# The gate product of the first attention moved ahead of the last convolution tap of q

## The reference, cut to what matters

```
q = _silu(x @ Wq); k = _silu(x @ Wk); v = _silu(x @ Wv); z = x @ Wz
q = _causal_dwconv(q, conv_q_w)          # 4 taps; k and v likewise
q = q * cos + rot_half(q) * sin          # k likewise
q = q / max(norm(q), 1e-12)              # k likewise
for s in range(4):                       # k, v and a, lagged by s tokens
    attn = sum_d(q * k_s) / sqrt(D)
    out = out + (attn * sigmoid(a_s * b))[..., None] * v_s
out = out * rsqrt(mean(out * out) + eps) * norm_w * _silu(z)
return out @ Wout
```

## Time and profile before

| | |
|---|---|
| median of 3 runs | 1179.99 us |
| profiled execution | 1189.32 us |
| its span | 1187.5 us |
| mean granted TensorE clock | 0.924 |
| TensorE matmuls busy | 1043.6 us, 88% of the span |
| VectorE busy | 750.1 us, 63% |
| ScalarE busy | 552.7 us, 47% |
| the product L1333 | 16 times, 112.2 to 436.6 us |

### The profile page before, as it was taken

The page is one execution under the profiler, slowest core; times in us unless marked ns, Lnnn a source line. Parts: engine busy times, 40 slices in busy tenths (PEclk is TensorE's granted clock), DMA queues, the critical chain, the costliest instruction groups (busy, mean ns, idle before and its releaser), DMA issues.

```text
span 1187.5 us, 16824 instructions
## 1 busy us (share of the span) xinstructions
PE 1043.6 (88%) x5771; PEld 819.4 (69%) x5771; DVE 750.1 (63%) x1275; ACT 552.7 (47%) x1081; POOL 285.7 (24%) x243
## 2 busy tenths in 40 slices
PE   6788999999999959847976999999997997669986
PEld 4567888888888844323434988998897454458775
DVE  1378998998989819953125787778776134523344
ACT  1056777777778648910113555555554021122220
POOL 0004234243243310022002112211210005336560
PEclk8589999999999969968997999999998998689997
DMA  7037778777677760060001111111100102168744
GB/s 259 1 86 155 165 157 167 156 158 173 153 152 168 186 139 10 1 186 9 0 0 46 36 54 53 45 34 53 53 0 0 67 1 75 52 204 257 248 154 183
DMA packets 77373, 121.59 MB, mean 102 GB/s; under 512 B 25027, under 2 KB 54414, under 8 KB 76560
## 3 DMA queue, kind: packets, MB, share of 16 engines
q1 hardware_dynamic: 65296, 86.91, 24.1%
q0 software_dynamic: 12032, 34.11, 15.0%
HBM read 70.31 MB, written 38.08 MB: 91 GB/s over the span
## 4 chain that ended last, share of the span: by engine, by line
PE 65%; DVE 19%; issue 6%; ACT 5%; DMA 3%; POOL 1%; DVEq 1%; another core or an unknown queue 0%; POOLq 0%; ACTq 0%; SPq 0%
PE psum L604 7%; PE psum L606 7%; PE psum L605 7%; PE psum L838 5%; PE psum L964 5%; DVE arena L1313 4%; PE psum L924 4%; PE psum L627 4%; PE psum L811 3%; PE psum L704 3%; PE psum L656 2%; DVE arena L1408 2%; PE psum L974 2%; PE psum L757 2%; PE psum L589 2%
## 5 line engine op out<-in xcount | busy, mean ns | idle before, releaser
L1313 DVE SCALAR_TENSOR_TENSOR arena<-arena,par_in 128x1024 f32<-128x1024 f32 x144 | 184.6, 1284 | 40.4 <-ACT arena L1041 28.2
L604 PE MATMUL psum<-lut_w_r,arena_r 128*128 128x512 f32 x320 | 132.0, 413 | 17.0 <-POOL arena_r L1739 10.1
L605 PE MATMUL psum<-lut_w_r,arena_r 128*128 128x512 f32 x320 | 127.7, 399 | 0.0
L606 PE MATMUL psum<-lut_w_r,arena_r 128*128 128x512 f32 x320 | 127.6, 399 | 0.0
L1723 POOL DMA_DIRECT2D arena<-arena x64 | 53.8, 983 | 216.5 <-DVE arena L1325 216.4
L1142 ACT ACTIVATE arena<-psum,small 128x256 f32<-128x256 f32 x128 | 59.4, 473 | 85.8 <-DVE small L1450 85.8
L1031 ACT ACTIVATE arena<-psum 128x1024 f32<-128x1024 f32 x48 | 49.3, 1027 | 73.9 <-PE psum L606 73.4
L604 PEld LDWEIGHTS psum<-lut_w_r,arena_r 128*128 128x128 f32 x320 | 61.3, 192 | 30.2 <-issue 10.1
L604 PE MATMUL psum<-arena_r 128*128 128x256 f32 x256 | 77.7, 304 | 1.5 <-DVE arena_r L1475 1.5
L1770 POOL DMA_INDIRECT out_rows<-arena x64 | 62.8, 981 | 51.6 <-issue 20.8
L1739 POOL TENSOR_TENSOR arena_r<-arena,arena_r 128x512 fp32r<-128x512 f32 x16 | 21.2, 1325 | 216.9 <-ACT arena_r L1153 216.9
(11 more groups left out here) (228 smaller groups left out, 2404.0 us busy)
## 6 DMA issues: line engine op xcount, KB each, us to landing
arena<-arena POOLq DMA_DIRECT2D x64, 256.0 KB, 5.6
arena<-in_w_moe SPq DMA_DIRECT2D x33, 384.0 KB, 7.2
slot_rows<-nowhere SPq DMA_DIRECT2D x16, 576.0 KB, 4.3
arena<-slot_rows SPq DMA_DIRECT2D x32, 288.0 KB
arena<-bands SPq DMA_DIRECT2D x16, 528.0 KB, 4.4
sq_rows<-arena POOLq DMA_DIRECT2D x16, 512.0 KB, 7.3
arena<-in_w_qkvz SPq DMA_DIRECT2D x16, 384.0 KB, 3.3
arena<-in_qkv_codes SPq DMA_DIRECT2D x16, 384.0 KB, 3.2
```

What stands on the lines that cost most here:

```text
L604: nc.tensor.matmul(dst, w_l, x_h, start=start, stop=False, skip_group_check=True)
L605: nc.tensor.matmul(dst, w_h, x_l, start=False, stop=False, skip_group_check=True)
L606: return nc.tensor.matmul(dst, w_h, x_h, start=False, stop=stop, skip_group_check=True)
L1313: nc.vector.scalar_tensor_tensor(by_batch(dst), by_batch(u[s])[:, :, j:j + S], par_in[:, bass.ds(M_CW + (w * H + h) * TAPS + j, 1)], by_ba ...
```

## The change

VectorE's three tap instructions for q are split: taps 1 and 2 come first, then the gate product, then tap 3. `conv` takes the taps to do as an argument; its calls for k and v stay as they were. The waits are the same ones: `a0_on` ahead of the product, the tap before ahead of each tap. The wait for tap 0 is now issued a second time, in front of tap 3, where it has long been met. Nothing changes in what is computed, on any other engine, or in any buffer.

```diff
-                def conv(w, s, dst):
+                def conv(w, s, dst, js=range(1, TAPS)):
                     dve.wait_ge(sg("a0_tap_" + s), h + 1)
-                    for j in range(1, TAPS):
+                    for j in js:
                         if j > 1:
                             dve.wait_ge(sg("a0_conv_" + s), 3 * h + j - 1)
                         nc.vector.scalar_tensor_tensor(by_batch(dst), by_batch(u[s])[:, :, j:j + S],
...
                 if 1 in st:
-                    conv(0, "q", cq)
+                    conv(0, "q", cq, range(1, TAPS - 1))
                 if 3 in st:
                     dve.wait_ge(sg("a0_on"), h - 1)
                     z = sz[1 - zq][par]
                     nc.vector.tensor_tensor(z, G[:, bass.ds((h - 2) * T, T)], z, ALU.mult).then_inc(sg("a0_g"), 1)
+                if 1 in st:
+                    conv(0, "q", cq, range(TAPS - 1, TAPS))
                 if 2 in st:
```

## The result

The changed kernel took 1171.07 us (median of 10 runs, 1165.82 to 1175.44) beside 1180.25 for the kernel before on the same chip (10 runs, 1174.36 to 1184.98). The ratio is 0.991, 95% interval 0.9885 to 0.9934: the changed kernel is faster, by 9.2 us by the medians and by 10.6 by the ratio, where 6.9 were forecast. All ratios from here on are a kernel's time over that of the kernel before, with the 95% interval in brackets. Two later measurements of the same kernel gave 0.9935 (0.9912 to 0.9958) and 0.9925 (0.9895 to 0.9955); the three, weighted by their intervals, have a mean of 0.9924 +- 0.0015, that is a gain of 9 us with 1.7 either way.

A forecast was written before the change was run, and what follows sets the result against it. TensorE was taken to bound each turn, with a short hole at the transposes. Closing it, 0.42 + 11 x 0.57 + 0.22 + 0.02 = 6.9 us, gave 1179.99 - 6.9 = 1173.1 us; range 1169.8 to 1177.2.

The forecast's parts named there:

- What bounds the kernel, and the hole: First attention's turns: TensorE's work plus one short hole, transposes L675 waiting for gate product L1333, 0.57 us lost.
- The size, turns 2 to 15: TensorE's hole closes: 0.42 in turn 2, 0.57 in each of turns 3 to 13, 0.22 and 0.02 after; 6.9 us.
- turn 2's 0.42: TensorE's hole ahead of the transposes in turn 2, counted as 0.42 us of the gain.
- The product's new place: VectorE: product follows tap 2, 1.42 us earlier; the `a0_on` signal comes 0.03 ahead of need, so its wait is costless.
- What is late next: VectorE starts q's taps 0.24 us late, 0.59 us idle remains ahead of k's taps; no new wait is due.
- Longer hole: Rival: TensorE could have started when its weight loads fell idle; gain 10.7 us, time 1169.3; chance 0.13.
- Slower: Rival: squares DMA L1711 lands late, at 9.7 us; each of 12 turns loses 1.2 us, time 1187.5; chance 0.04.
- The page's price: Comparison: at the page's matmul beat k's 12 matmuls are 0.2 us shorter, the hole as much longer; 14 turns sum to 9.7.

## Why the prediction was right and wrong

*What bounds the kernel, and the hole.* Right. The hole was the only spare time that TensorE had in a turn; with it closed TensorE is busy without a break, and L675 is gone from the table of waits. Rows 4 and 5 sufficed.

*The size, turns 2 to 15.* Here the term was mis-sized on which the forecast hung: "So the gain is TensorE's hole", 0.57 in each of turns 3 to 13 and 6.9 in all. In all seven traces of versions with the product behind tap 1 or 2 in every turn, the stretch from turn 2 to 15 is 276.92 to 276.93 us; in both of the kernel before it is 284.25 and 284.29. That is 7.33 to 7.36 less, where the sum without turn 2's 0.42 had 6.5; with turn 2's hole it is 7.7 to 7.8 us (ratio 0.9934). The missing term is some 0.06 us in each turn, and it lies behind the hole: in the kernel before, v's first matmul came 0.85 us behind the first transpose, and with the hole closed 0.79. The rows give the likely reason: after a wait the first weight load and the first transpose began at the same moment (245.07), and with the wait gone the load runs 0.24 us ahead, under k's last matmul. The sum took the hole to end where the first transpose starts. Turns 14 and 15, written down with 0.22 and 0.02, gave 0.27 and 0.11 in the first two traces.

*The rest of the first measurement, and the range.* 9.2 us (medians) or 10.6 (ratio) were measured and 7.8 are explained. With 7.8 the forecast would have been 1172.2, inside the range; what put the time outside is the rest, which no trace of the changed stretch shows. The kernel's other parts vary by more than that from one execution to the next, in kernels with the same code there: up to turn 2, 107.6 to 114.8 us; from the transposes of turn 16 to those of 17, 19.7 to 22.3; from the first of the experts' matmuls (L964) to the end, 131 to 137. The first three runs of before, 0.6 us apart, hid this, though the profiled execution, 9.3 us above their median, could have warned; the range was made from the unknown costs alone. The kernel before itself ran from 1174.4 to 1185.0. 7.8 us (0.9934) lies inside the interval of each single measurement but the edge of the first, which it touches, and inside that of their mean, 0.9909 to 0.9939. Yet the four other versions with the same 276.93 us came out at 0.9909 to 0.993, all on the same side of 0.9934, though three of them share their runs of the kernel before. Whether the last microsecond of 9.0 is chance or a small gain elsewhere stays open.

*The product's new place.* Right: the wait for `a0_on` cost nothing, at 0.03 us of margin by the sum; the version between taps 1 and 2 shows that over a microsecond of it would have been free too. The version ahead of all taps shows the price one place further, and that the user of the low parts, z's projection, has to be on the list.

*What is late next.* Right in kind, with more room than forecast: VectorE's q taps start right behind the sines, 0.04 to 0.16 us late (0.24 forecast), and the idle ahead of k's taps is 0.84 us in turns with L1346 (0.59 forecast) and 1.32 without. The version with half of the turns shows that the lag is real.

*The rivals.* "Longer hole" gave 1169.3, the nearest to the first measurement, but not for its reason: the hole by the weight loads, 10.7 us, was never gained, and every trace of the changed stretch shows 7.3 to 7.4 from turn 2 to 15. That its time was met is luck. The weight load does seem to matter, but only by the 0.06 us a turn. "Slower", by the squares DMA, did not come in the steady turns. In turn 16 ScalarE waits 8.5 to 9.1 us for that DMA before v_tok in the traces before and after, and not in the version that moves it.

*The page's price.* By the beat of 216 ns that the Trainium skill (TensorE: Matmul & The Clock Gate, the section "Wait — 56ns, not 53.3ns?") states for 512 columns, the prediction estimated 9.7 us. The float32r matmuls of the projections follow one another after 0.233 us on average in the traces of both kernels, so the measurement decides against that estimate for the profiled executions, and its nearness to the measured gain is chance.

## What to carry to other kernels

Where one engine is busy but for a hole at one wait, closing it gains the time from the last instruction's beat to the start of the waiting one, and a little more behind it (here 0.06 us for each of TensorE's waits). Compare the steps behind a wait with the same steps where nothing waited. Move the producer no further than the hole asks for: its neighbours come later by it, and each of their users must be followed to the engine that reads it. Before giving a range, look at how the untouched parts vary between executions; three equal runs don't show it. Two markers around the changed stretch repeated to 0.04 us in two traces of the same kernel whose spans differ by 10.5.

## What was not expected of the hardware

After 6.5 us without a matmul the scores met a granted clock of 0.50 and took 3.86 us, and 2.05 at 1.00 with the gap filled. With the squares DMA moved the gap was only 3.8 us, and the scores took 3.86 as well, again at 0.50. Behind such idle stretches, the level that a short group of matmuls meets changed from one execution to the next here: L719 of turn 16 took 2.05 us in two traces of the changed kernel and 3.78 in the third.

The last rotation DMA of turn 16 was late by a DMA issued behind it on the same queue: it landed after 9.3 us with the squares DMA behind it, and the one trace in which that was moved shows at most 6.6 us. Moving the index loads changed nothing (9.3 us).
